# Two-layer decoder on one core: keys and queries of a head group moved in turn, first parts cast by ScalarE, three stand-in products for eight

## The reference

```python
q, k, v = x @ Wq, src @ Wk, src @ Wv      # per head 16 wide; src is x (D) or the context (B, E)
scores = q @ k.T / sqrt(16)                # D: causal, E: masked
out = softmax(scores) @ v @ Wo
```

## Time and profile before

| what | us |
|---|---|
| median of 3 runs (4395.07 to 4396.11) | 4395.63 |
| the profiled execution | 4399.94 |
| its span, first to last instruction | 4398.2 |
| PE busy | 3843.8 (87%) |
| DVE busy | 2449.9 (56%) |
| ACT busy | 1681.6 (38%) |
| transfers on the SP queue, share of 16 engines | 20.0% |
| mean granted TensorE clock | 0.934 |

### The profile page before, as it was taken

How to read it: one execution, slowest core, us unless ns; L and a number is a source line. 1 busy time by engine, 2 the same in 40 slices (tenths; PEclk the granted TensorE clock), 3 DMA queues, 4 the chain that set the end, 5 groups by cost and what they waited for, 6 DMA issues and landing times.

```text
span 4398.2 us, 57319 instructions
## 1 busy us (share of the span) xinstructions
PE 3843.8 (87%) x21938; PEld 1843.6 (42%) x21938; DVE 2449.9 (56%) x6073; ACT 1681.6 (38%) x2508; POOL 152.0 (3%) x168
## 2 busy tenths in 40 slices
PE   5778888999977888899987798889998879888999
PEld 2342444345434244435533424443553442443355
DVE  5457566742356756673236575657324667665632
ACT  2644433431264542352136354235113636422511
POOL 1000020000000001000000001100000000200000
PEclk9998999999999998899998999889999889988999
DMA  5213002122421201202241210120315121012031
GB/s 191 96 31 60 17 18 48 22 87 75 129 75 37 45 17 42 45 1 101 65 161 44 41 36 17 42 45 1 105 61 161 49 45 27 18 42 45 1 112 59
DMA packets 134702, 254.40 MB, mean 58 GB/s; under 512 B 23268, under 2 KB 82660, under 8 KB 128996
## 3 DMA queue, kind: packets, MB, share of 16 engines
q1 hardware_dynamic: 134408, 250.50, 20.0%
HBM read 156.04 MB, written 44.04 MB: 45 GB/s over the span
## 4 chain that ended last, share of the span: by engine, by line
PE 66%; DVE 16%; ACT 7%; SPq 5%; issue 3%; DMA 2%; POOL 0%; DVEq 0%; POOLq 0%; ACTq 0%
PE ps L1207 11%; PE ps L578 7%; PE ps L1225 5%; DVE mx L732 5%; PE ps L561 5%; SPq L429 5%; PE ps L506 4%; PE ps L1543 3%; DVE ps L729 3%; PE ps L1461 3%; PE ps L402 3%; ACT a_X L1616 2%; PE ps L566 2%; PE ps L1485 2%; DMA a_fin<-scores 2%
## 5 line engine op out<-in xcount | busy, mean ns | idle before, releaser
L670 ACT ACTIVATE PT<-ps 128x1024 f32<-128x1024 f32 (+3 forms) x640 | 604.8, 958 | 473.1 <-PE ps L566 243.6
L506 PE MATMUL ps<-KS,QS 96*128 96x512 bf16 (+3 forms) x1280 | 469.3, 406 | 114.6 <-DVE mx L732 53.5
L732 DVE TENSOR_REDUCE mx<-ps 128x1 f32<-128x512 f32 (+3 forms) x768 | 437.8, 619 | 169.0 <-PE ps L506 82.7
L1207 PE MATMUL ps<-xnT,f_w 128*128 128x512 f32 x1088 | 490.9, 595 | 0.0
L561 PE MATMUL ps<-QS,KS 99*128 99x512 bf16 (+2 forms) x1280 | 429.7, 381 | 6.7 <-ACT QS L660 6.2
L729 DVE CUSTOM_DVE_ANT_0 ps<-ps,mneg 128x512 f32<-128x512 f32 x512 | 342.2, 715 | 133.0 <-PE ps L506 131.3
L578 PE MATMUL ps<-PT,VP 128*32 128x512 f32 (+3 forms) x2560 | 386.5, 588 | 14.2 <-ACT OT L681 13.9
L1313 DVE TENSOR_TENSOR f_tm<-f_si,ps 128x512 f32<-128x512 f32 x128 | 88.1, 688 | 493.2 <-ACT f_si L1265 493.1
L1265 ACT ACTIVATE f_si<-ps 128x512 f32<-128x512 f32 x136 | 80.8, 597 | 596.6 <-PE ps L1220 577.5
L506 PEld LDWEIGHTS ps<-KS,QS 96*128 96x128 bf16 x1280 | 131.2, 103 | 414.1 <-DVE mx L732 195.8
L1207 PEld LDWEIGHTS ps<-xnT,f_w 128*128 128x128 f32 x1088 | 206.9, 191 | 204.9 <-issue 198.4
(11 more groups left out here) (266 smaller groups left out, 5416.5 us busy)
## 6 DMA issues: line engine op xcount, KB each, us to landing
f_w<-in_wF SPq DMA_DIRECT2D x136, 384.0 KB, 3.1
scores<-a_fin SPq DMA_DIRECT2D x64, 256.0 KB, 3.0
a_fin<-scores SPq DMA_DIRECT2D x16, 1024.0 KB, 8.5
a_Y<-in_wA SPq DMA_DIRECT2D x5, 3072.0 KB, 14.9
KS<-KP SPq DMA_DIRECT2D x240, 64.0 KB, 2.5
scores<-a_fin SPq DMA_DIRECT2D x64, 192.0 KB, 3.0
a_fin<-scores SPq DMA_DIRECT2D x16, 768.0 KB, 4.3
a_fin<-scores SPq DMA_DIRECT2D x24, 512.0 KB, 3.6
```

The costliest lines, as they stand in the source:

```text
L506: last = nc.tensor.matmul(o, m["QS"][0:KR, h, i * P:(i + 1) * P], m["KS"][0:KR, h, f:f + w], start=True, stop=not c.causal)
L670: nc.scalar.activation(m["PT"][:, mp % 2, j % 2, :, 0:w], ps[:, b0:b0 + 2, 0:w], ACT.Exp, scale=HD ** -0.5).then_inc(g("exp"), 1)
L732: nc.vector.tensor_reduce(m["mx"][:, h % 2, i, f // BANK:f // BANK + 1], ps[:, k % 2, 0:w], AX.X, ALU.max, negate=True).then_inc(g("slot_f ...
L1207: last = nc.tensor.matmul(ps[:, 2 * v + e % 2, :], m["w"][:, e % NRING, (2 * v + k) * P:(2 * v + k + 1) * P], xnT[:, k, :], start=(k == 0) ...
```

## The change

Three things change, in all three stages or in some of them.

- `moves`: K0, Q0, K1, Q1, K2, Q2 in place of K0, K1, Q0, Q1, K2, Q2.
- `cast_by_act`: in B for K and Q, in E for K alone, ScalarE writes the first bf16 part from PSUM directly, in front of its copy to `val`. VectorE waits for it and leaves its first cast out. D is not touched by this.
- `WARM_STACK` is 3.

```diff
-        self.moves = [(kind, t, gr) for t in range(2) for kind, gr in (("k", 0), ("k", 1), ("q", 0), ("q", 1), ("k", 2), ("q", 2))]
+        self.moves = [(kind, t, gr) for t in range(2) for kind, gr in (("k", 0), ("q", 0), ("k", 1), ("q", 1), ("k", 2), ("q", 2))]
...
+    def cast_by_act(self, kind):
+
+        return self.cross and (kind == "k" or not self.masked)
...
-WARM_LN, WARM_T, WARM_STACK = 22, 6, 8
+WARM_LN, WARM_T, WARM_STACK = 22, 6, 3
...
                 o = m["val"][:, e % NVAL, :]
+                if c.cast_by_act(kind):
+                    top = m["QP"][:, 0, t, :] if kind == "q" else m["KP"][:, 0, t, f * BANK:(f + 1) * BANK]
+                    if c.masked:
+                        nc.scalar.activation(top, ps[:, c.bank(e), :], ACT.Identity, bias=bkE[:, t:t + 1]).then_inc(g("cast"), 1)
+                    else:
+                        nc.scalar.activation(top, ps[:, c.bank(e), :], ACT.Copy).then_inc(g("cast"), 1)
...
-            def parts(dst, src, rest, last_sem):
-
-                ch.link(nc.vector.tensor_copy(dst(0), src))
+            def parts(dst, src, rest, last_sem, cast=False):
+
+                if not cast:
+                    ch.link(nc.vector.tensor_copy(dst(0), src))
                 ch.link(nc.vector.tensor_tensor(rest, src, dst(0), ALU.subtract))
...
-                parts(dst, m["val"][:, e % NVAL, :], m["rest"][:, :], g("split"))
+                if c.cast_by_act(kind):
+                    dve.wait_ge(g("cast"), e + 1)
+                parts(dst, m["val"][:, e % NVAL, :], m["rest"][:, :], g("split"), c.cast_by_act(kind))
```

More of the change, by code:

```diff
@@ L298, in decoder @@
             if c in STAGES:
-                for n in ("proj", "val", "split", "v_mm", "v_up", "v_zero", "k_ones", *(f"stack_in{gr}" for gr in GROUP_AT.values()), "slot_mm", "slot_free",
+                for n in ("proj", "cast", "val", "split", "v_mm", "v_up", "v_zero", "k_ones", *(f"stack_in{gr}" for gr in GROUP_AT.values()), "slot_mm", "slot_free",
                           "m_parts", "m_mm", "m_row", "st_mm", "exp", "pv", "o_up", "recip", "y_mm"):
```

## The result

The changed kernel took 4380.77 us in the median of 11 runs (4377.08 to 4399.93), the kernel before 4392.88 in 11 runs beside it (4381.43 to 4402.5). The ratio is 0.9976, with a 95% interval of 0.9966 to 0.9987: 10.5 us less (5.7 to 14.9), or 0.24%. The forecast was 4384, 11.3 less than the 4395.63 of its three runs of before.

A forecast was written before the change was run, and what follows sets the result against it. TensorE carries 66% of the span, mostly untouched; waits on SP's transfers bind in B and D, stand-ins in E. B -9.4, E -5.2, D +3.3 give -11.3 us from the median 4395.63: 4384, range 4374 to 4396.

The forecast's parts named there:

- B, order, casts and stand-ins: In attention stage B, first maximum 2.55 us earlier, less 0.2 for the clock: -2.35 per stage, -9.4 us over four rounds.
- The inner account: In B: the cut of stand-ins is worth 0.9 us; without the casts moved, VectorE would be free 1.4 later.
- E: In attention stage E, five stand-ins fewer save 6.4 us over four rounds, less 1.2 for the clock: -5.2 us.
- D: In attention stage D, the new order idles SP's queue 0.82 us, delaying the copy into OT: +3.3 us over four rounds.
- Sum: Whole kernel: -9.4 - 5.2 + 3.3 = -11.3 us, giving 4384 us; chance 0.52.
- (1): B and E: the clock takes back the earlier start, about 1.3 us per stage; 4395 us, no measurable change; chance 0.20.
- (2): First scores of B and E: the stand-ins held the clock, so fewer cost 25 us; 4410 us, slower; chance 0.06.
- (3): D: the queue's gap costs nothing, the transfers and not their issue being the limit; 4381 us; chance 0.10.
- (4): Half of B and E: the clock comes back a step earlier, 4 x 1.6 us less; 4378 us; chance 0.12.

## Why the prediction was right

**B, order, casts and stand-ins (-2.35 per stage).** Right. Forecast: first score 19.9, first maximum 20.5; measured 19.6 and 20.2. The 0.3 come from two terms. The projection of the first Q tile was let slip by 0.18 and did not: its cast starts 11.39 us after the stage's start (331.71 less 320.32), where `val` started before. And the cast and `val` were put one behind the other at 0.60 each, while they start 0.49 apart. So Q's parts were ready 0.35 sooner. The stand-ins did not slip either, and with 0.66 for three they are done at 19.6 and not 19.8. Over the five profiled kernels that have all three parts in B, B's mean length is 173.7 against 176.1 in the one profile of before: -2.4. Of the 2.8 gained at the first maximum 0.4 went to the clock by these means; the forecast took off 0.2, a size that no row gave. The inner account holds too. Stand-ins: forecast 0.9 at TensorE, measured 0.9 at the maximum (21.1 and 20.2). Casts: the forecast says 1.4, though its own rows give 1.2 (345.70 less 344.5); measured 1.4 at the maximum. Order: 1.9 at the maximum (22.1 and 20.2). They don't add, since each only uncovers the next latest.

**E (-1.3 per stage).** Right in its cause, with some luck in the size. The first maximum moved from 27.6 (29.3 in rounds 3 and 4) to 26.5. In rounds 1 and 2 the first score came 1.08 earlier (27.17 and 26.10), the 5 x 0.216 of the forecast. The forecast took 2.13 for rounds 3 and 4, as if the stand-ins stayed at the lower level there; they ran at the upper one, and the move was 2.8. On the other side, rounds with stand-ins at the lower level are rarer than the one profile of before had shown: 3 of 16 in the four profiles with eight. So in the mean of these four and of the eight profiles with three the first maximum moved by 1.1, and the forecast had 1.6 less 0.3 for the clock. In the profile of the changed kernel E lost 2.6 per stage, since before had the two rounds at the lower clock and after none. Over the 8 profiles with three stand-ins E's mean is 201.0, over the 4 with eight 202.3: -1.35. SP stands for 3.2 us, as said (3.1), and it stays hidden: the copy into OT waits for TensorE there.

**D (+0.82 per stage).** Right at the point. The copy into OT moved from 63.8 (mean of 6 profiles with the old order) to 64.4 (5 with the new), +0.67. The lengths moved by +0.4 (117.5 and 117.9), half of the forecast and within a scatter of 2 us. The changed kernel itself shows +1.05, with 113 us at the lower level in its four D and 102 before. The forecast named a longer spell as a bound.

**Sum.** By these means 4 x (-2.4 - 1.35 + 0.4 to 0.67) is -12.3 to -13.4; forecast -11.3, measured -10.5 (-14.9 to -5.7). The measurement bears out the direction and the size of the sum. Its interval is too wide to test the single terms; these rest on the points inside the stages.

**The rivals.** (1), the start given back to the clock, is not what happens on average with all three parts, but it is real. B of round 4 kept only 1.9 of its 2.8 us, at a clock of 0.91, and the kernels with the order or the casts alone kept next to nothing of 1.4 and 0.9 us in B. The forecast had no term that tells these cases apart. (2) is real as a mechanism and small: fewer stand-ins, a lower clock, in either order. With all three parts the earlier start outweighs it. That the closed gap is the reason fits the profiles of B and is not shown for the whole kernel. The forecast had argued against it with E of round 3, which was not the place where it shows. (3) fell: the copy into OT moves by 0.8 us with the gap, and by 6.6 or 8.3 with a second queue. (4) is part of the scatter: in E of the changed kernel the spell at 1.2 GHz takes 24 us in every round, in E with the old order in D alone 27 in every round.

**What stays open.** Why the clock's low spells in B and E last from 20 to 34 us was not settled; it makes stages of equal work differ by up to 3 us, and effects under 5 us are hidden in the whole kernel's time. Whether three stand-ins are better than none or eight is not settled either.

## What to carry to other kernels

When several things can be the last to be ready, work out each one's time and read their order: here transfers, stand-ins and VectorE lay within 3 us, and each change alone was worth nothing that could be measured. A stage that waits for the end of a queue turns every idle moment of the queue into time, whatever is gained in front; shorten the queue first, if need be by letting an idle engine issue. Stand-in products cost their own time and hold the clock a little; in B too few of them in front of an open gap made the slow spell longest, so close the gap first, then cut them, and measure the clock over many runs. A single profile can be the slowest run of its kernel.

## What the runs showed of the hardware

- Two queues issue almost independently: ScalarE's 12 transfers took 7.74 us (0.645 each) and its 18 further ones 11.81 (0.66 each), beside SP's 30 in 19.87 (0.66 each), where one queue alone took 0.635.
- Two activations of 0.60 from the same PSUM bank start 0.49 apart.
- The granted clock differs between rounds with the same instructions. At the same first maximum B took 172.4 to 175.2 us, and whole runs of one kernel spread by 20 us and more.
- The stand-ins ahead of the scores raise the mean granted clock: 0.9301 with none, 0.9315 with three, 0.9353 with eight, over 11 or 12 runs each.
